# Twelve 1 MB weight loads per chunk issued from ScalarE's DMA queue, one step after their step on SyncE

## What is computed

```
x = x + 0.5 * ffn(layernorm(x))
x = x + mamba(layernorm(x))
x = x + 0.5 * ffn(layernorm(x))

ffn:   r = sigmoid(xr @ W_r.T);  k = relu(xk @ W_k.T)**2;  out = r * (k @ W_v.T)
       (xr, xk mix each token with the one before it)
mamba: xs, z = split(xn @ W_in.T);  xc = silu(conv4(xs))
       dt, B, C = split(xc @ W_xproj.T);  delta = softplus(dt @ W_dt.T + b_dt)
       h_t = exp(delta * A) * h_(t-1) + delta * B * xc;  y = C . h_t + D_skip * xc
       out = (y * silu(z)) @ W_out.T + residual
```

## Time and profile before

| What | Value |
|---|---|
| Median of three runs | 4679.0 us (4676.57 to 4679.5) |
| The profiled execution: its time | 4679.25 us |
| The profiled execution: its span, first to last instruction | 4677.5 us |
| TensorE, VectorE busy | 90%, 90% |
| ScalarE, GpSimd busy | 68%, 76% |
| Mean granted TensorE clock | 0.974 |
| DMA | 810.7 MB, 173 GB/s |

### The profile page before, as it was taken

The page is one execution under the profiler, slowest core; times in us unless marked ns, Lnnn a source line. Parts: engine busy times, 40 slices in busy tenths (PEclk is TensorE's granted clock), DMA queues, the critical chain, the costliest instruction groups (busy, mean ns, idle before and its releaser), DMA issues.

```text
span 4677.5 us, 58356 instructions
## 1 busy us (share of the span) xinstructions
PE 4190.6 (90%) x16768; PEld 2358.7 (50%) x16768; DVE 4202.4 (90%) x3266; ACT 3164.0 (68%) x6740; POOL 3559.8 (76%) x3712
## 2 busy tenths in 40 slices
PE   5777999999999999999999999999999999999787
PEld 2444555555555555555455555555555555555453
DVE  1799999999999999999999999999999999999991
ACT  3666677767767677667767767776776767766562
POOL 2677787877878778787788878787787887878771
PEclk8888999999999999999999999999999999999798
DMA  2455555555655555565555655556565555655551
GB/s 76 125 158 185 177 180 181 178 195 167 192 180 178 173 181 195 181 194 177 182 173 181 198 177 180 181 178 195 168 192 181 178 176 182 193 179 167 159 184 55
DMA packets 423058, 810.74 MB, mean 173 GB/s; under 512 B 41265, under 2 KB 41265, under 8 KB 418641
## 3 DMA queue, kind: packets, MB, share of 16 engines
q1 hardware_dynamic: 422736, 807.00, 54.1%
HBM read 772.25 MB, written 34.60 MB: 172 GB/s over the span
## 4 chain that ended last, share of the span: by engine, by line
PE 45%; DVE 24%; issue 12%; POOL 8%; ACT 7%; DMA 3%; SPq 0%; DVEq 0%; POOLq 0%; ACTq 0%
DVE decay L1099 13%; PE mm L478 9%; PE y_acc L573 9%; PE mm L489 8%; DVE g L1107 7%; POOL dbx L1306 6%; PE mm L515 5%; PE mm L500 4%; PE mm L602 3%; DVE xc L1051 3%; DMA c_all<-bc_scratch 3%; PE mm L525 3%; PE mm L537 2%; POOL xin L1295 1%; PE mm L464 1%
## 5 line engine op out<-in xcount | busy, mean ns | idle before, releaser
L1306 POOL TENSOR_TENSOR dbx<-u,b_all 128x1024 f32<-128x1024 f32 x1024 | 2417.9, 2361 | 187.0 <-DVE g L1107 183.6
L1099 DVE TENSOR_TENSOR_SCAN decay<-decay,state,dbx 128x1024 f32<-128x1024 f32 x1024 | 2406.9, 2350 | 155.2 <-ACT decay L913 131.7
L1107 DVE TENSOR_TENSOR g<-decay,c_all 128x1024 f32<-128x1024 f32 x1024 | 1246.3, 1217 | 57.7 <-PE y_acc L573 45.0
L573 PE MATMUL y_acc<-ident,g 128*128 128x128 f32 x8192 | 1077.8, 279 | 238.2 <-DVE g L1107 235.8
L573 PEld LDWEIGHTS y_acc<-ident,g 128*128 128x128 f32 x8192 | 950.3, 143 | 657.9 <-DVE g L1107 384.8
L910 ACT ACTIVATE decay<-delta,neg_a 128x512 f32<-128x512 f32 x1024 | 708.5, 692 | 37.1 <-ACT state L919 0.4
L919 ACT ACTIVATE state<-decay 128x2 f32<-128x2 f32 x1024 | 167.9, 164 | 782.5 <-DVE g L1107 780.0
L913 ACT ACTIVATE decay<-delta,neg_a 128x511 f32<-128x511 f32 x1024 | 687.1, 671 | 0.0
L500 PE MATMUL mm<-wbuf_c,col 128*128 128x512 f32 x1024 | 458.2, 593 | 9.6 <-ACT delta L861 8.2
L1051 DVE SCALAR_TENSOR_TENSOR xc<-mm,conv_sb,xc 128x509 f32<-128x509 f32 (+2 forms) x384 | 285.3, 743 | 50.4 <-ACT xs_last L825 41.4
L500 PEld LDWEIGHTS mm<-wbuf_c,col 128*128 128x128 f32 x1024 | 187.4, 190 | 214.7 <-issue 212.5
(11 more groups left out here) (107 smaller groups left out, 5377.0 us busy)
## 6 DMA issues: line engine op xcount, KB each, us to landing
b_all<-bc_scratch SPq DMA_DIRECT2D x1024, 256.0 KB, 3.7
c_all<-bc_scratch SPq DMA_DIRECT2D x1024, 256.0 KB, 4.0
wbuf_d<-in_w_r SPq DMA_DIRECT2D x32, 1024.0 KB, 7.1
wbuf_c<-in_w_v SPq DMA_DIRECT2D x32, 1024.0 KB, 7.7
xin<-in_x SPq DMA_DIRECT2D x16, 1024.0 KB, 7.0
wbuf_c<-in_w_k SPq DMA_DIRECT2D x16, 1024.0 KB, 5.6
wbuf_d<-in_w_in SPq DMA_DIRECT2D x16, 1024.0 KB, 8.2
res_scratch<-rows SPq DMA_DIRECT2D x16, 1024.0 KB, 6.2
```

The costliest lines, as they stand in the source:

```text
L573: last = pe.matmul(y_acc[:, tb, j * P:(j + 1) * P], g[:, s % PAIRS, j, tb * P:(tb + 1) * P], ident[:, :], start=n == 0 and j == 0 and tb % ...
L1099: dve.tensor_tensor_scan(d, d, flat(dbx[:, s % DBX, :, :]), state[:, batch, s, 0:1], ALU.mult, ALU.add).then_inc(scan_done, 1)
L1107: dve.tensor_tensor(g[:, s % PAIRS, :, :], decay[:, s % PAIRS, :, :], c_all[:, s % CRING, :].unsqueeze(1).broadcast_to([P, QT, W]), ALU.mu ...
L1306: pool.tensor_tensor(dbx[:, s % DBX, :, :], u[:, q % 2, :, :], b_all[:, s % BRING, :].unsqueeze(1).broadcast_to([P, QT, W]), ALU.mult).the ...
```

## The change

The twelve weight loads leave SyncE's program and stand in ScalarE's, in a new function `load_weights`. It is called at each step right after `make_decay`, ahead of everything else of that step. Each load stands one step later than on SyncE (`LOAD[...] + 1`), and keeps the same wait on TensorE's progress, now made by ScalarE. The loads of x, B, C and the residual, and all stores, stay on SyncE. The diff, with loads that repeat the pattern left out:

```diff
--- before.py
+++ after.py
@@ -366,9 +363,6 @@
-                    if back and s == LOAD["wo1"]:
-                        after(mark(z_pe, b, "7"))
-                        sp.dma_start(wbuf["b"][:, :, :], piece(w_out, 512, 0)).then_inc(wo_loaded[1], 16)
...
@@ -427,20 +384,6 @@
-                    if ahead and s == LOAD["wk0"]:
-                        if back:
-                            after(mark(f_pe[1], b, "v3"))
-                        elif scn:
-                            after(mark(z_pe, it, "3"))
-                        elif front:
-                            after(mark(f_pe[0], f, "v3"))
-                        sp.dma_start(wbuf["c"][:, :, :], piece(w_k, 0, 0)).then_inc(wk_loaded[0], 16)
...
@@ -918,6 +861,73 @@
+            def load_after(sem_and_count):
+                act.wait_ge(*sem_and_count)
...
+            def load_weights(it, s):
+                scn, front, back, ahead = has(it, 0), has(it, 1), has(it, -1), has(it, 2)
+                f, b = it + 1, it - 1
+                if back and s == min(LOAD["wo1"] + 1, NSTEP - 1):
+                    load_after(mark(z_pe, b, "7"))
+                    act.dma_start(wbuf["b"][:, :, :], piece(w_out, 512, 0)).then_inc(wo_loaded[1], 16)
...
+                if back and s == min(LOAD["wr1"] + 1, NSTEP - 1):
+                    if front:
+                        load_after(mark(m_pe, f, "xs3"))
+                    elif due(count := f_pe[1].at(b - 1, "r3")):
+                        load_after((f_pe[1].sem, count))
+                    act.dma_start(wbuf["d"][:, :, :], piece(w_r, 0, 0)).then_inc(wr_loaded[1], 16)
...
+                if scn and s == min(LOAD["wz1"] + 1, NSTEP - 1):
+                    if back:
+                        load_after(mark(f_pe[1], b, "k3"))
+                    act.dma_start(wbuf["b"][:, :, :], piece(w_in, 0, E + 512)).then_inc(wz_loaded[1], 16)
+                if ahead and s == min(LOAD["wr0"] + 1, NSTEP - 1):
+                    if back:
+                        load_after(mark(f_pe[1], b, "r3"))
+                    elif front:
+                        load_after(mark(m_pe, f, "xs3"))
+                    act.dma_start(wbuf["d"][:, :, :], piece(w_r, 0, 0)).then_inc(wr_loaded[0], 16)
+                if ahead and s == min(LOAD["wk0"] + 1, NSTEP - 1):
+                    if back:
+                        load_after(mark(f_pe[1], b, "v3"))
+                    elif scn:
+                        load_after(mark(z_pe, it, "3"))
+                    elif front:
+                        load_after(mark(f_pe[0], f, "v3"))
+                    act.dma_start(wbuf["c"][:, :, :], piece(w_k, 0, 0)).then_inc(wk_loaded[0], 16)
+
@@ -931,6 +941,7 @@
                     if scn:
                         make_decay(it, s)
+                    load_weights(it, s)
```

More of the change, by code:

```diff
@@ L309, in tokens_of @@
                 return dram[batch, bass.ds((k - batch) * (W // BATCHES), W), :].rearrange("(t p) d -> p t d", p=P)
-            def piece(dram, rows0, cols0):
-                return dram[rows0:rows0 + 512, cols0:cols0 + 512].rearrange("(t p) n -> p t n", p=P)
             for i, v in ((0, mu_r), (1, mu_k), (4, ln_w), (5, ln_b)):
@@ L400, in body @@
                                      flat(rows[1][:, :, :])).then_inc(res_stored, 16)
[L401 to L419, removed]
                     if front and s == LOAD["bc_out"]:
@@ L429, in body @@
                         sp.dma_start(xin[:, :, :], tokens_of(x, it + 2, (bt + 2) % BATCHES)).then_inc(x_loaded, 16)
-                    if ahead and s == LOAD["wr0"]:
-                        if back:
-                            after(mark(f_pe[1], b, "r3"))
-                        elif front:
-                            after(mark(m_pe, f, "xs3"))
-                        sp.dma_start(wbuf["d"][:, :, :], piece(w_r, 0, 0)).then_inc(wr_loaded[0], 16)
-                    if ahead and s == LOAD["wk0"]:
-                        if back:
-                            after(mark(f_pe[1], b, "v3"))
-                        elif scn:
-                            after(mark(z_pe, it, "3"))
-                        elif front:
-                            after(mark(f_pe[0], f, "v3"))
-                        sp.dma_start(wbuf["c"][:, :, :], piece(w_k, 0, 0)).then_inc(wk_loaded[0], 16)
                     if back and s == LOAD["out"]:
@@ L919, in save, with piece, mark @@
                 act.activation(state[:, batch, s, :], decay[:, s % PAIRS, :, W - 1], ACT.Copy).then_inc(saved, 1)
+            def piece(dram, rows0, cols0):
+                return dram[rows0:rows0 + 512, cols0:cols0 + 512].rearrange("(t p) n -> p t n", p=P)
+            def load_after(sem_and_count):
+                act.wait_ge(*sem_and_count)
+            def mark(marks, k, name):
+                return marks.sem, marks.at(k, name)
+            def load_weights(it, s):
[4 more added lines that the diff above has]
+                    act.dma_start(wbuf["b"][:, :, :], piece(w_out, 512, 0)).then_inc(wo_loaded[1], 16)
+                if front and s == min(LOAD["wv0"] + 1, NSTEP - 1):
+                    load_after(mark(f_pe[0], f, "k3"))
+                    act.dma_start(wbuf["c"][:, :, :], piece(w_v, 0, 0)).then_inc(wv_loaded[0], 16)
+                if front and s == min(LOAD["wxs0"] + 1, NSTEP - 1):
+                    load_after(mark(f_pe[0], f, "r3"))
+                    act.dma_start(wbuf["d"][:, :, :], piece(w_in, 0, 0)).then_inc(wxs_loaded[0], 16)
+                if scn and s == min(LOAD["wz0"] + 1, NSTEP - 1):
+                    load_after(mark(f_pe[0], f, "v3") if front else mark(f_pe[1], it - 2, "v3"))
+                    act.dma_start(wbuf["c"][:, :, :], piece(w_in, 0, E)).then_inc(wz_loaded[0], 16)
+                if back and s == min(LOAD["wk1"] + 1, NSTEP - 1):
+                    load_after(mark(y_pe, b, "o3"))
+                    act.dma_start(wbuf["b"][:, :, :], piece(w_k, 0, 0)).then_inc(wk_loaded[1], 16)
+                if front and s == min(LOAD["wxs1"] + 1, NSTEP - 1):
+                    if back:
+                        load_after(mark(y_pe, b, "o3"))
+                    elif due(m_pe.at(f - 1, "xs7")):
+                        load_after(mark(m_pe, f - 1, "xs7"))
+                    act.dma_start(wbuf["a"][:, :, :], piece(w_in, 0, 512)).then_inc(wxs_loaded[1], 16)
+                if back and s == min(LOAD["wv1"] + 1, NSTEP - 1):
+                    load_after(mark(z_pe, it, "3") if scn else mark(f_pe[1], b - 1, "v3"))
+                    act.dma_start(wbuf["c"][:, :, :], piece(w_v, 0, 0)).then_inc(wv_loaded[1], 16)
+                if back and s == min(LOAD["wr1"] + 1, NSTEP - 1):
[4 more added lines that the diff above has]
+                    act.dma_start(wbuf["d"][:, :, :], piece(w_r, 0, 0)).then_inc(wr_loaded[1], 16)
+                if scn and s == min(LOAD["wo0"] + 1, NSTEP - 1):
+                    if front:
+                        load_after(mark(m_pe, f, "xs7"))
+                    elif back:
+                        load_after(mark(y_pe, b, "o3"))
+                    act.dma_start(wbuf["a"][:, :, :], piece(w_out, 0, 0)).then_inc(wo_loaded[0], 16)
+                if scn and s == min(LOAD["wz1"] + 1, NSTEP - 1):
[9 more added lines that the diff above has]
+                if ahead and s == min(LOAD["wk0"] + 1, NSTEP - 1):
+                    if back:
+                        load_after(mark(f_pe[1], b, "v3"))
[4 more added lines that the diff above has]
+                    act.dma_start(wbuf["c"][:, :, :], piece(w_k, 0, 0)).then_inc(wk_loaded[0], 16)
```

## The result

The changed kernel takes 4700.07 us (median of four runs, 4698.74 to 4703.72) against 4677.78 us for the kernel before on the same chip (four runs, 4674.07 to 4679.5). The ratio is 1.005 with a 95% interval of 1.0033 to 1.0067: 22.3 us slower. The forecast was 4705 us, slower, with a range of 4684 to 4722. The profiled execution of the changed kernel took 4698.74 us, its span is 4696.7 us, and the mean granted TensorE clock is 0.975. One of the ten executions of the first experiment's kernel took 16461.69 us, a slow run; its ratio is over the other nine.

What follows compares the result with a forecast made beforehand. It took a chain alternating between VectorE's scan and multiply and TensorE's projections as the bound. Terms 21 + 0 + 0 + 2 + 2.5 = 25.5 us gave a span of 4703.0, plus 1.75 around it: 4705 us, range 4684 to 4722.

Steps and rivals of the forecast that it cites:

- The wait of wk0: ScalarE, step 57: wk0's load waits for the last v matmul, making a scan 1.6 us late 13 times, 21 us.
- The bounds of 1.2 and 2.2 us: Limits per late scan: 1.2 if TensorE's slack takes part (16 us), 2.2 if an issue takes 1 us (29 us).
- Issues on ScalarE: DMA issues, notably before softplus at steps 4 and 54, are hidden behind running activations: 0 us.
- rival 1: Issues not hidden: each holds ScalarE's activations about 0.4 us; at two softplus places 12 us more, 4717 us; chance 0.22.
- The bound of 12 us: Cost if issues before softplus are not hidden: 30 x 0.4 us.
- wo1's landing: wo1, issued later, still lands before TensorE's out projection needs it: 0 us, bounded by 1 us in 15 chunks.
- SyncE's side: Issues and waits removed from SyncE, and B and C loads freed from its weight loads: 0, bounds 0 to -12.7 us.
- The 12.7 us that C rows could give: Cap on the gain from earlier C rows: VectorE's multiply idles 57.7 us, 45.0 of it for TensorE.
- rival 4: Faster: C rows' landing is on the chain, 14 pieces of about 8.3 us; 60 us go, 4645 us; chance 0.07.
- Start: First loads: wr0 and wk0 on ScalarE's own queue get in among x's packets, making x about 2 us late.
- End: Iteration 16: wr1 stands behind mix activations on ScalarE and lands late for the r matmuls, 2.5 us.
- Rival 3: VectorE or TensorE makes up the 1.6 us stall; only start and end cost stay, 4684 us; chance 0.13.

Runs made afterwards that it cites:

- the first experiment: The changed kernel with wk0 issued by SyncE at step 56 again, the other eleven loads left on ScalarE: 4678.21 us, ratio 0.9999.
- the run with the wait alone: The kernel before, all loads on SyncE, with ScalarE also waiting for the last v matmul at step 57 and issuing nothing: 4696.33 us, ratio 1.0039.
- the six more issues: The changed kernel plus six 2 KB loads into an unused tile at steps 4 and 54, right ahead of softplus: 4805.44 us, ratio 1.027.

## Why the prediction was right, point by point

- **The wait of wk0, 21 us.** Right in place, count and size: 13 waits of 6.1 us (about 6 was named), 1.59 us each in the scans against 1.6, sum 20.7. The working also had the issue of 0.38 us behind the wait on the path; the run with the wait alone shows 0.46 for it. That VectorE gives next to nothing back is shown by 39.85 of 40.00 us; it was 1.0 us in all, at step 62. The bounds of 1.2 and 2.2 us were not needed. The sentence that the save would begin 3.8 us later holds: 6.12 us of idle in place of 2.38 is 3.7 more.
- **Issues on ScalarE, 0.** Right, and rival 1 fell: eleven loads on ScalarE take the time of before. One detail was off. I looked for the issue inside a running L913, the last activation of the decay; it begins with the first. The bound of 12 us had the wrong shape as well: the six more issues show that cost is not per issue but per issue beyond the activations in flight.
- **wo1's landing, 0.** Right, and in part by luck. The landing grew from 6.5 to 7.6 us, and 1.1 us was the margin given. Issued 0.68 us ahead of L853's end, it came just in time in 15 chunks and 0.2 us late in one. On the rule that an engine takes turns between queues with work (the Trainium skill, "DMA: Bandwidth & Descriptors", section "Queues, rings and completion order"), the trace agrees in part: wo1 lands in 7.6 us in place of 6.5, and wk0 in 8.7 in place of 5.6, but wk1 lands in 5.5 in place of 7.9 and the second xs load in 5.2 in place of 6.7. For wk0 the queue and the step together make it: 8.7 us with wk0 alone on ScalarE, 5.5 with wk0 alone on SyncE. No run separates the turns from other causes of slower landings.
- **SyncE's side, 0.** Right. The 12.7 us that C rows could give were not to be had, and rival 4 fell: the chain's 14 pieces on C rows vanished with no gain. The 57.7 us of idle time before the multiply was the better guide than the chain's 3%.
- **Start, +2.** Wrong. The step that failed is that wr0 and wk0 would get in among x's packets: x, issued at 6.58 us, landed 7.16 us later, against 7.60. Even that is no gain of the change: with the loads on ScalarE the landing takes 7.14 to 7.76 us in the traces, and in two kernels with the start of the kernel before it takes 7.46 (the wait without the load) and 6.58 (wk0 at step 62). I looked at the first use of the queue and not at the first scan, where wk0 stood ahead of the B rows. That gave 1.9 us, of which the first C row took back 1.7.
- **End, +2.5.** Wrong: 0. I took wr1 to be issued when ScalarE reaches it in order. It was issued before six activations that stand ahead of it.
- **The sum.** The span was 4696.7 us against 4703.0. 4.5 us of cost at the two edges did not come, and wk0's place and the first C row together gave 0.2. The late scans give 1.0 us back at step 62, 0.08 a chunk; this is there in every kernel with the stall at step 58 and in none without it. The rest are differences that the change is not shown to make: 1.3 us less before the first scan, 1.7 less at step 60, 2.2 more at step 5 and 0.7 more elsewhere. So the main term carries the forecast, and that the total came so near it is in part luck. The 2.2 us at step 5 come from values of both signs, and about 1 us up and down at this step appears also in the runs that took the time of before. I put them down to TensorE's clock, below, by their size alone.
- **Rival 3**, a stall that is absorbed, fell with the 20.7 us at step 58.

## What to carry to other kernels

A DMA moved to a compute engine brings its wait with it, and the wait is the price. Find the moment at which its semaphore is met, and put the load where the engine would wait at least that long for something else, or behind that moment: one step decided between 0, 22 and 102 us here. The issue itself was free while ScalarE had activations in flight or idle time to come; behind an unmet wait with work due, and beyond the activations in flight, it was paid in full. Before trusting a landing margin, look at the time between the two steps on the engine that issues now, since its steps are not equally long.

## What the runs showed of the hardware that was not expected

- **The queue runs far ahead.** ScalarE's queue issued a load 0.68 us before the first of three activations ahead of it ended, and in the last chunk before six of them had started. It stops at an unmet wait: the load wk0 was issued at 2640.85 us, 0.03 us after the matmul that it waits for, and 5.66 us after the last activation ahead of it.
- **TensorE's clock falls behind short idle times.** At steps 3 and 4 of some chunks, in both kernels, the granted clock is 0.50 (1.2 GHz) after an idle time of 2.62 us of TensorE. Two stretches of the changed kernel, iteration 14, with the columns as above:

```profile
4074.00:4076.00 2.00, 0.46 (x3) 0.46 (x4) 2.00 (x3) 1.97 (x5) 2.00 (x1) 0.92 0.05 18
4076.00:4078.00 2.00, 2.00 (x8) 1.54 (x7) 2.00 (x2) 1.97 (x5) 1.92 (x4) 0.50 0.17 37
```

  The same idle time in iteration 8 of the kernel before was followed by a clock of 1.00 (from 2392 to 2394 us). Where it is 0.50, the dt matmuls end later and softplus waits: the table load at 4079.50 us had been held 1.33 us by L492. The idle time before the first table load of softplus at this step is 4.5 us in all 16 chunks before and 7.3 after. In the runs with late scans or late weights the loss was larger than the wait itself, and the low clock stood beside it.
- **Issues in a row are longer than one**: of the six small loads the first takes 0.35 us in the median and the others 0.45 to 0.55; in the chunk shown four take 2.63 us.
